# Two 64-row tiles for the score matmuls of a head pair, and value matmuls in bursts of eight

## The reference

```python
qc = q - q.mean(axis=-1, keepdims=True)
kc = k - k.mean(axis=-1, keepdims=True)
cov = jnp.einsum('bhsd,bhtd->bhst', qc, kc) / D
q_var = jnp.var(q, axis=-1, ddof=1)
k_var = jnp.var(k, axis=-1, ddof=1)
scores = cov + q_var[..., :, None] * k_var[..., None, :] / D
attn = jax.nn.softmax(scores, axis=-1)
out = jnp.einsum('bhst,bhtd->bhsd', attn, v)
```

## Time and profile before

| | |
|---|---|
| median of three runs | 1313.66 us |
| span of the profiled execution | 1312.0 us |
| its time against the median | the span and 1.66 us around it |
| TensorE busy (matmuls) | 1219.3 us, 93% |
| VectorE busy | 1059.6 us, 81% |
| ScalarE busy | 960.6 us, 73% |
| GpSimd busy | 312.5 us, 24% |
| chain that ended last | TensorE 62%, ScalarE 18%, VectorE 8% |

### The profile page before, as it was taken

The page is one execution under the profiler, slowest core; times in us unless marked ns, Lnnn a source line. Parts: engine busy times, 40 slices in busy tenths (PEclk is TensorE's granted clock), DMA queues, the critical chain, the costliest instruction groups (busy, mean ns, idle before and its releaser), DMA issues.

```text
span 1312.0 us, 35299 instructions
## 1 busy us (share of the span) xinstructions
PE 1219.3 (93%) x12100; PEld 783.7 (60%) x12100; DVE 1059.6 (81%) x3074; ACT 960.6 (73%) x1696; POOL 312.5 (24%) x510
## 2 busy tenths in 40 slices
PE   2699999999999999999768999999999999999998
PEld 1456666555656566565335666676666676666676
DVE  5888888888888888888457887888887888887873
ACT  1388898888888898888756667776667776667744
POOL 4334433343333433341120111110111110111000
PEclk9899999999999999999869999999999999999999
DMA  3000000000000000000010000000000000000000
GB/s 94 5 15 15 14 17 17 17 13 13 17 17 13 13 17 17 17 14 15 17 29 17 26 10 17 24 24 24 24 8 16 24 24 24 24 4 20 17 10 16
DMA packets 50855, 24.93 MB, mean 19 GB/s; under 512 B 6384, under 2 KB 50288, under 8 KB 50800
## 3 DMA queue, kind: packets, MB, share of 16 engines
q1 hardware_dynamic: 50800, 24.21, 6.6%
HBM read 15.28 MB, written 8.39 MB: 18 GB/s over the span
## 4 chain that ended last, share of the span: by engine, by line
PE 62%; ACT 18%; issue 9%; DVE 8%; ACTq 1%; DMA 1%; SPq 1%; POOL 1%; DVEq 0%; POOLq 0%
PE bank L515 54%; ACT Kexp L1353 6%; PE bank L546 4%; ACT hmid L1438 4%; ACT prob L1331 3%; DVE smax L1002 2%; PE bank L596 2%; ACT prob L1364 1%; DVE prob L1006 1%; ACT KT L1322 1%; PE bank L615 1%; DMA x_in<-in_L_attn_x 1%; ACT oT L1272 1%; ACT feat L1286 1%; DVE Vexp L994 1%
## 5 line engine op out<-in xcount | busy, mean ns | idle before, releaser
L924 DVE TENSOR_REDUCE rowmax<-bank 128x2 f32<-128x512 f32 x512 | 336.7, 685 | 59.5 <-PE bank L515 56.3
L1331 ACT ACTIVATE prob<-bank 128x512 f32<-128x512 f32 x512 | 294.0, 601 | 29.2 <-PE bank L515 24.6
L515 PEld LDWEIGHTS bank<-w_sb,hmid 128*128 128x128 f32 x2048 | 244.0, 192 | 23.7 <-issue 11.7
L1438 ACT ACTIVATE hmid<-bank,up_scale 128x512 f32<-128x512 f32 x256 | 176.2, 733 | 110.1 <-PE bank L515 109.9
L515 PE MATMUL bank<-w_sb,hmid 128*128 128x128 f32 x2048 | 248.2, 276 | 0.0
L1353 ACT ACTIVATE Kexp<-bank,head_bias,head_mask 128x512 f32<-128x512 f32 x256 | 188.2, 848 | 42.5 <-PE bank L515 42.5
L515 PE MATMUL bank<-QT,KT 128*128 128x256 bf16 x1024 | 197.3, 275 | 10.2 <-ACT prob L1331 7.1
L515 PE MATMUL bank<-KT,QT 128*128 128x256 bf16 x1024 | 200.4, 279 | 5.7 <-DVE rowmax L924 5.1
L1222 DVE SCALAR_TENSOR_TENSOR acc<-bank,gate,acc 128x128 f32<-128x128 f32 x512 | 143.3, 342 | 72.3 <-PE bank L515 70.2
L515 PE MATMUL bank<-prob,V 128*9 128x256 f32 x2048 | 159.6, 384 | 0.0
L1322 ACT COPY KT<-bank 64x1024 bf16<-64x1024 bf16 x128 | 128.8, 1007 | 27.6 <-PE bank L546 23.1
(11 more groups left out here) (164 smaller groups left out, 1846.6 us busy)
## 6 DMA issues: line engine op xcount, KB each, us to landing
x_in<-in_L_attn_x SPq DMA_DIRECT2D x32, 128.0 KB, 2.1
QT<-shiftT SPq DMA_DIRECT2D x256, 2.0 KB
z_scratch<-z_out SPq DMA_DIRECT2D x32, 128.0 KB, 1.8
xg<-in_L_attn_x SPq DMA_DIRECT2D x64, 64.0 KB, 1.9
zg<-z_scratch SPq DMA_DIRECT2D x64, 64.0 KB, 2.0
out<-acc SPq DMA_DIRECT2D x64, 64.0 KB, 1.7
w_sb<-in_L_ffn_w SPq DMA_DIRECT2D x1, 1024.0 KB, 6.8
in_wT<-in_L_ffn_in_proj_w SPq DMA_DIRECT2D x1, 192.0 KB, 2.4
```

The source lines that it names most:

```text
L515: return pe.matmul(o, l, r, start=start, stop=stop, skip_group_check=True)
L924: dve.tensor_reduce(rowmax[h // 8][:, :, h % 2, h % 8 // 2], row_scores[h % 3][:].rearrange("p (s t) -> p s t", s=ST), AX.X, ALU.max).then ...
L1331: act.activation(prob[:, h % 8].rearrange("p t s -> p (t s)"), col_scores[h % 2][:], ACT.Exp, scale=1.0 / D).then_inc(s_exp, 1)
L1438: act.activation(hmid[e % 2][c][:], up_bank[c][:], ACT.Gelu, scale=up_scale[:, 0:1]).then_inc(s_mid, 1)
```

## The change

- Keys are kept once: `KT[p]` has both heads of a pair, one in rows 0 to 63, the other in rows 64 to 127. `k_out` is one copy of 128 rows instead of two of 64, in slots 3 and 12, and the clears of KT go.
- Score matmuls contract over 64 rows. Column and row pass of a slot alternate, instruction by instruction, and the row pass takes the other head of the pair (`row_head`), so that neighbours use different halves of the array. Their waits (`col_ready`, `row_ready`) now all stand ahead of the slot's first matmul. VectorE takes the maxima in the same swapped order of heads.
- The two halves of the value matmuls of four heads are one burst, at the end of slots 6, 9, 13 and (for heads 12 to 15) slot 1 of the next step, behind what `PE_AT` puts in the slot.

```diff
+PE_PV = (6, 9, 13, 1)
...
+def row_head(i):
+
+    return i ^ 1
...
-        KT = [[sb(f"KT{p}_{a}", [P, PAIRS, NS], BF16) for a in range(2)] for p in range(2)]
+        KT = [sb(f"KT{p}", [P, PAIRS, NS], BF16) for p in range(2)]
...
-            def row_pass(n, p, h):
-                if h % 8 == 0:
-                    pe.wait_ge(s_qt[h // 8], n + 1)
-                    pe.wait_ge(s_kt[h // 8], n + 1)
-                if h == 0:
+            def head_rows(h):
+
+                return slice(STACK * (h % 2), STACK * (h % 2 + 1)), h // 2
+
+            def row_ready(n, i):
+                if i % 8 == 0:
+                    pe.wait_ge(s_qt[i // 8], n + 1)
+                    pe.wait_ge(s_kt[i // 8], n + 1)
+                if i == 0:
                     if positive(H * n):
                         pe.wait_ge(s_max, H * n)
-                elif h >= 3:
-                    pe.wait_ge(s_max, H * n + h - 2)
-                q = h // 2
-                for st in range(ST):
-                    ins = mm(row_scores[h % 3][:, st * NS:(st + 1) * NS],
-                             QT[p][:, q, st * P:(st + 1) * P], KT[p][h % 2][:, q, :])
-                ins.then_inc(s_row, 1)
-
-            def col_pass(b, p, h):
+                elif i >= 3:
+                    pe.wait_ge(s_max, H * n + i - 2)
+
+            def row_pass(n, p, i, st):
+                rows, q = head_rows(row_head(i))
+                ins = mm(row_scores[i % 3][:, st * NS:(st + 1) * NS],
+                         QT[p][rows, q, st * P:(st + 1) * P], KT[p][rows, q, :])
+                if st == ST - 1:
+                    ins.then_inc(s_row, 1)
...
+            def col_ready(b, h):
                 if h % 8 == 0:
                     pe.wait_ge(s_shd[h // 8], 64 * (b + 1))
                 if positive(H * b + h - 1):
                     pe.wait_ge(s_exp, H * b + h - 1)
-                q = h // 2
+
+            def col_pass(b, p, h, tc):
+                rows, q = head_rows(h)
+                ins = mm(col_scores[h % 2][:, tc * NS:(tc + 1) * NS],
+                         KT[p][rows, q, tc * P:(tc + 1) * P], QT[p][rows, q, :])
+                if tc == ST - 1:
+                    ins.then_inc(s_col, 1)
+
+            def pv(b, p, g):
+                pe.wait_ge(s_exp, H * b + 4 * g + 4)
+                if g == 0 and positive(b):
+                    pe.wait_ge(s_ot[1], b)
+                if g == 2:
+                    pe.wait_ge(s_ot[0], b + 1)
                 for tc in range(ST):
-                    ins = mm(col_scores[h % 2][:, tc * NS:(tc + 1) * NS],
-                             KT[p][h % 2][:, q, tc * P:(tc + 1) * P], QT[p][:, q, :])
-                ins.then_inc(s_col, 1)
-
-            def pv(b, p, g, tc):
-                if tc == 0:
-                    pe.wait_ge(s_exp, H * b + 4 * g + 4)
-                    if g == 0 and positive(b):
-                        pe.wait_ge(s_ot[1], b)
-                    if g == 2:
-                        pe.wait_ge(s_ot[0], b + 1)
-                for j in range(4):
-                    h = 4 * g + j
-                    ins = mm(pv_bank[32 * j:32 * j + FEAT, (g % 2) * NS:(g % 2 + 1) * NS],
-                             V[p][:, tc, h, :], prob[:, h % 8, tc, :],
-                             start=(tc == 0), stop=(tc == ST - 1))
-                if tc == ST - 1:
-                    ins.then_inc(s_pv, 1)
+                    for j in range(4):
+                        h = 4 * g + j
+                        ins = mm(pv_bank[32 * j:32 * j + FEAT, (g % 2) * NS:(g % 2 + 1) * NS],
+                                 V[p][:, tc, h, :], prob[:, h % 8, tc, :],
+                                 start=(tc == 0), stop=(tc == ST - 1))
+                ins.then_inc(s_pv, 1)
...
-                        col_pass(b, p, h)
-                    for tc in range(ST):
-                        if h == tc and prev:
-                            pv(b - 1, 1 - p, 3, tc)
-                        if h % 4 == 1 + tc and h > 4 and cur:
-                            pv(b, p, h // 4 - 1, tc)
+                        col_ready(b, h)
+                    if nxt:
+                        row_ready(b + 1, h)
+                    for half in range(ST):
+                        if cur:
+                            col_pass(b, p, h, half)
+                        if nxt:
+                            row_pass(b + 1, 1 - p, h, half)
...
-                    if nxt:
-                        row_pass(b + 1, 1 - p, h)
...
+                    if h == PE_PV[3] and prev:
+                        pv(b - 1, 1 - p, 3)
+                    for g in range(3):
+                        if h == PE_PV[g] and cur:
+                            pv(b, p, g)
...
+                h = row_head(i)
                 dve.tensor_reduce(rowmax[h // 8][:, :, h % 2, h % 8 // 2],
-                                  row_scores[h % 3][:].rearrange("p (s t) -> p s t", s=ST),
+                                  row_scores[i % 3][:].rearrange("p (s t) -> p s t", s=ST),
...
-                for t in (*KT[0], *KT[1], stack):
-                    dve.memzero(t[:]).then_inc(s_dve, 1)
-                    dve.wait_ge(s_dve, own.next())
+                dve.memzero(stack[:]).then_inc(s_dve, 1)
+                dve.wait_ge(s_dve, own.next())
...
-            def k_out(n, p, k, a):
-                if isinstance(n, int) and n == 0:
-                    act.wait_ge(s_zeroed, 1)
-                if a == 0:
-                    act.wait_ge(s_kt_ps[k], n + 1)
-                    if positive(H * (n - 2) + 8 * k + 8):
-                        act.wait_ge(s_col, H * (n - 2) + 8 * k + 8)
+            def k_out(n, p, k):
+                act.wait_ge(s_kt_ps[k], n + 1)
+                if positive(H * (n - 2) + 8 * k + 8):
+                    act.wait_ge(s_col, H * (n - 2) + 8 * k + 8)
                 ps = misc[1 - k][:].bitcast(BF16).rearrange("p (q s) -> p q s", q=HP)
-                half = slice(HP * k, HP * (k + 1))
-                rows = slice(a * STACK, (a + 1) * STACK)
-                ins = act.copy(KT[p][a][rows, half, :], ps[rows])
-                if a == 1:
-                    ins.then_inc(s_kt[k], 1)
+                act.copy(KT[p][:, HP * k:HP * (k + 1), :], ps).then_inc(s_kt[k], 1)
```

More of the change, by code:

```diff
@@ L917, in q_out, with take_max @@
                                 misc[0][:].bitcast(BF16).rearrange("p (q s) -> p q s", q=HP)).then_inc(s_qt[k], 1)
-            def take_max(n, h):
-                dve.wait_ge(s_row, H * n + h + 1)
-                if h % 8 == 0:
+            def take_max(n, i):
+                dve.wait_ge(s_row, H * n + i + 1)
+                if i % 8 == 0:
                     if positive(n):
-                        dve.wait_ge(s_shift[h // 8], n)
+                        dve.wait_ge(s_shift[i // 8], n)
+                h = row_head(i)
                 dve.tensor_reduce(rowmax[h // 8][:, :, h % 2, h % 8 // 2],
-                                  row_scores[h % 3][:].rearrange("p (s t) -> p s t", s=ST),
+                                  row_scores[i % 3][:].rearrange("p (s t) -> p s t", s=ST),
                                   AX.X, ALU.max).then_inc(s_max, 1)
@@ L1376, in step @@
                         shift_out(b, 1)
-                    if nxt:
-                        for a in range(2):
-                            if h == ACT_AT["k1"] + a:
-                                k_out(b + 1, 1 - p, 1, a)
+                    if h == ACT_AT["k1"] and nxt:
+                        k_out(b + 1, 1 - p, 1)
                     if h == ACT_AT["v"] and nxt:
@@ L1392, in step @@
                         copy_out(b, 0)
-                    if prep:
-                        for a in range(2):
-                            if h == ACT_AT["k0"] + a:
-                                k_out(b + 2, p, 0, a)
+                    if h == ACT_AT["k0"] and prep:
+                        k_out(b + 2, p, 0)
                     first_head(b, h)
```

## The result

The changed kernel takes 1317.52 us (median of 20 runs, 1315.07 to 1322.21); the kernel before, run beside it, takes 1313.92 (20 runs, 1312.42 to 1317.02). The ratio is 1.0027, with a 95% interval of 1.0018 to 1.0036: 3.6 us slower. The forecast was 9.3 us slower, so the direction held and the size did not.

A forecast was written before the change was run, and what follows sets the result against it. Hand-overs between engines were taken as the bound: a step of 18.75 instead of 18.42 us adds 10.2 over 31 steps, the start gives back 1.0; span 1321.2, with 1.66 around it 1323 us, range 1290 to 1345.

The forecast's parts named there:

- The bound: Middle of the score stage: hand-overs between engines decide, not busy shares, though TensorE is busy 417.5 of 423.6 us.
- What the change takes away: Per step: scores 3.5 us by side-by-side streaming, value matmuls 0.8, key copies 2.0; KT clears nothing.
- Switches: TensorE changes tiling between scores and transposes or projections eleven times a step, 0.10 us each, 1.1 a step.
- The ring: Chain of last-arriving links from one z_out to the next in the score loop: 18.75 us a step against 18.42.
- the first ring: Score-loop path from z_out through exponentials, features, burst and a key copy to the next z_out: 18.75 us.
- the second: Score-loop path by VectorE, through its maxima and the copy of QT back to slot 0's scores: 18.63 us.
- Where it turns: Slot 1: burst moves behind features' wait; TensorE idles about 1.5 us before shift transposes, ScalarE about 1 before oT.
- Start and end: Start gains 1.0 us from one key copy gone; end steps without row passes cost nothing, under 1 us without cover.
- the clock as a rival: TensorE's granted clock falling as its busy share drops to about 77%: unlikely, put with the slow cases (12%).
- The rings don't close: Score loop bound by VectorE: step 16.4 us, time 1250, or 17.25 and 1276; chance 20%.
- Switches free, or twice as dear: Tiling changes on TensorE at 0 or 0.2 us: 1316 or 1338 us; chances 13% and 12%.
- No overlap: Score matmuls on the two array halves don't stream together: 19.85 us a step, 1357 us; chance 10%.

The follow-up runs named there:

- e8: Kernel before, with ScalarE's second copy of the transposed keys issued behind the exponential of slot 4 instead of slot 3: 1330.67 us, ratio 1.0127.
- e2: Changed kernel with row and column pass of a slot on the same head, so the same 64 array rows: 1347.78 us, ratio 1.0260.
- e1: Changed kernel with slot 1's burst of heads 12 to 15 moved ahead of the QT and shift transposes: 1285.24 us, ratio 0.9781 to before.
- e4: Kernel before with only the four value-matmul bursts added, its scores and key copies left alone: 1338.84 us, ratio 1.0196.
- r_after: Changed kernel run once more, unchanged, for a second profile: 1318.88 us, one execution.
- e6: Changed kernel with column-pass score matmuls of heads 0 and 1 of the last batch issued five more times each: 1315.44 us, ratio 1.0013.
- the tiles alone: Changed kernel's scores and single KT, with value matmuls put back into halves in their old slots: 1277.45 us, ratio 0.9730 to before.

## Why the prediction was right in direction and wrong in size

*The bound.* Right as far as it was tried: a wait that lands on TensorE in the kernel before lengthens the step (e8).

*What the change takes away.* Right: four score matmuls take 0.23 us, and e2 shows the overlap as the cause. The bound "side by side" was the true one. TensorE's work was to fall by 3.2 us a step (17.6 to 14.4); as busy time it fell by 2.7 (18.15 to 15.4).

*Switches.* Right at S6, 0.32 from S6 to the transposes (304.19 to 304.51), as 0.22 and 0.10. Between the shift transposes and the burst, the ring counted 0.21 and it is 0.11 (299.64 to 299.75), which is most of the 0.12 by which that link was too long.

*The ring.* The step of the prediction that failed is a mis-sized term, the pair of ScalarE stretches, "z_out to the exponential of slot 13, ScalarE without a gap: 2.80" and "oT, shift, two exponentials, one key copy, to the exponential of slot 4: 2.93". They measure 2.61 each, 0.51 together. I had subtracted starts of before and read the absence of a bracketed wait as the absence of waits. The rows of the changed kernel show the sign I missed. Work that is ready starts about 0.1 us ahead of the end of the one before it, as the key copy does at 302.58, though the exponentials run from 301.62 to 302.68; in the kernel before it starts 0.1 us behind their end. In the kernel before the stretch from the exponentials of slots 2 and 3 to the key copy is 1.16 where it is 0.96 now, and from the copy of oT to the shift 0.59 where it is 0.48. The key copies, one in each stretch, look as if they waited for their transposes there. TensorE and ScalarE of the kernel before, both places:

```profile
301.95 0.61 PE L546 MATMUL bank<-identb,stack 128*128 128x128 bf16 x8
...
302.68 1.01 ACT L1322 COPY KT<-bank 64x1024 bf16<-64x1024 bf16 x1
...
311.77 1.05 PE L546 MATMUL bank<-identb,stack 128*128 128x128 bf16 x16 [0.19 <-issue]
...
312.86 1.01 ACT L1322 COPY KT<-bank 64x1024 bf16<-64x1024 bf16 x1
```

The transposes end at 302.56 and 312.82, 0.12 and 0.04 us before the copies start. In the changed kernel they end earlier (at 301.89 for the copy at 302.58, at 312.24 for that at 312.46). The shift copy of before starts 0.11 us behind its transposes too (300.86 + 0.28, and 301.25). The key copies make 0.38 of the 0.51 (0.20 and 0.18), the shift copy 0.11. That these are waits is read from the times and was not tried by itself. A duration taken where the engine that is the bound is waited for can hold some of that wait, though no gap of ScalarE shows it.

Three links were forecast 0.35 too short together, above all in three places: the projection by Wo to z_out took 1.30 instead of 1.20, from an exponential to its scores passed 0.71 or 0.72 instead of 0.67, and the switch from transposes into a burst took 0.15 instead of 0.10. So the sum was 0.28 high: 0.05 us a step over before instead of 0.33, 1.6 us instead of 10.2 if all 31 steps had it.

That the direction held was partly luck. With the two stretches and the shift transposes right and the three short links as forecast, the first ring is 18.75 - 0.51 - 0.12 = 18.12 and the second 18.63 - 0.32 - 0.12 = 18.19, both below the 18.42 of before, and the same working would have said about 8 us faster.

*Where it turns.* Right, and the larger effect by far: e1 shows that the burst behind the wait for features costs 0.97 us a step, and e4 that the bursts lose on their own. The prediction named this place and its two waits (about 1.5 and about 1 us forecast, 1.27 and 0.79 read), and ScalarE's wait ahead of the exponential of slot 7 (about 1, and 1.23 read).

*Start and end.* The start was to give 1.0. The first z_out is 0.6 us earlier in one profile and 0.4 later in the other (r_after), so no gain is shown. The end was costed at nothing, with a bound of 1 us, and that was wrong: step 31 takes 5.5 us more. The prediction saw the clock as a rival, "a fall is unlikely", from a row with TensorE 78% busy. The row was that of the kernel before, and at the place where the changed kernel is 51% busy no row of before could speak for it. e6 shows that the clock makes most of those 5.5 us in the profile (4.6, from 27.1 to 22.5); in the median it is about 1.8 us, by intervals that overlap.

*The sum.* The first profile adds up, z_out by z_out: 0.6 us won up to the first, 0.6 lost from there to 605.0 (1.2 in the loop, the rest won back on its two sides), 1.3 won in step 30 and 5.5 lost in step 31, together the 4.2 by which the last is later. The medians differ by 3.6. How these split is not shown: 1.6 for the loop and about 1.8 for the clock come near it, and that they do may be chance.

*Rivals.* "The rings don't close" fell at 18.47. Its number, 1276 at a step of 17.25, is nearly that of the tiles alone (1277.45, 17.21): where the burst does not stand behind the features, the step does go there. Whether VectorE then bounds it was not tried; it is busy for 389.7 of 424 us in that run. "Switches free, or twice as dear" fell at 0.10, and "No overlap" at 0.23 us for four score matmuls.

## What to carry to other kernels

When an engine is made faster inside a loop of three engines, write down the ring of hand-overs from one step's mark to the next and look for what now stands behind a wait: here the place of one burst was worth nine times the net effect of the change, and the bursts took back all that the tiles gained. Take the links' durations from stretches where nothing waits for the engine that is the bound, and compare the start of the next instruction with the end of the last. Check the releaser that a row names against the waits in the code. At the end of a stage, where work thins out, look at the granted clock before costing it at nothing.

## What the hardware showed that was not expected

- After six microseconds (624 to 630 us) with TensorE busy for 3.04 the granted clock stood at 0.50 for twelve more, and a pair of 512-column fp32 matmuls took 2.07 us instead of 1.13. Twenty matmuls that compute nothing new, put into two waits, kept it at 1.00 up to 642 us and made step 31 shorter (22.5 us instead of 27.1).
- Score matmuls on different halves of the array overlap even when they are not neighbours in the program. With both passes of a slot in one half, the eight matmuls of slots 0 and 1 still take 0.46 us, and the first of slot 1 starts together with the first of slot 0 (x2 at 291.74 us, e2).
- The change of tiling between the shift transposes (16 columns) and the value matmuls (9 columns, each in a tile) costs nothing to be seen: 0.11 us for two transposes of 128 columns. From the row tiles to the full array it costs 0.10 (0.32 from S6 to the transposes, less the 0.22 of two passes before).
- The changed kernel spreads over 7.1 us in twenty executions, with a mean granted clock of 0.983 at 1315.07 us and 0.976 at 1322.15; the kernel before spreads over 4.6.
